# Grouped attention of a fused transformer kernel: query tiles, dense sums, output halves and the last value blocks are made and evicted in other units

## The reference

```python
GROUPS, HPG, KVC = (4, 4, 128)
q = jnp.einsum('bsh,he->bse', x, w_q).reshape(b, sq, GROUPS, HPG, KVC)
kv = jnp.einsum('bsh,he->bse', x, w_kv)
k, v = jnp.split(kv, 2, axis=-1)
scores = jnp.einsum('bqgpd,bkgd->bgqpk', q, k) * SCALE
scores = jnp.where(causal[None, None, :, None, :], scores, -jnp.inf)
probs = jax.nn.softmax(scores, axis=-1).astype(x.dtype)
ctx = jnp.einsum('bgqpk,bkgd->bqgpd', probs, v).reshape(b, sq, HEADS * KVC)
return jnp.einsum('bse,eh->bsh', ctx, w_dense)
```

## Time and profile before

| What | us |
|---|---|
| median of 3 runs | 998.9 (996.7 to 1003.71) |
| the profiled execution's own time | 998.63 |
| its span, first to last instruction | 996.6 |
| grouped attention in it, first scores to last unit's exponentials | 597.0 to 919.3 |
| PE, DVE, ACT busy over the span | 899.9, 744.6, 577.8 |
| granted TensorE clock, mean | 0.991 |

### The profile page before, as it was taken

The page is one execution under the profiler, slowest core; times in us unless marked ns, Lnnn a source line. Parts: engine busy times, 40 slices in busy tenths (PEclk is TensorE's granted clock), DMA queues, the critical chain, the costliest instruction groups (busy, mean ns, idle before and its releaser), DMA issues. The chain is left out here.

```text
span 996.6 us, 19557 instructions
## 1 busy us (share of the span) xinstructions
PE 899.9 (90%) x7309; PEld 601.5 (60%) x7334; DVE 744.6 (75%) x1803; ACT 577.8 (58%) x1102; POOL 173.7 (17%) x131
## 2 busy tenths in 40 slices
PE   3999989999999999999998988899999989998897
PEld 2787743334433433468876765676666766766686
DVE  7846877888888888245468666888888888888654
ACT  5534223566666766744446546767676666766263
POOL 4010130052344145000014500000000000000154
PEclk9999999999999999999999999999999999999999
DMA  5020343453255330203101003667776676766101
GB/s 117 1 88 0 110 122 61 77 104 70 57 107 92 66 77 24 66 1 112 58 1 43 0 1 64 128 120 119 118 122 119 107 132 114 122 123 122 25 1 43
DMA packets 176918, 75.60 MB, mean 76 GB/s; under 512 B 154648, under 2 KB 172744, under 8 KB 175304
## 3 DMA queue, kind: packets, MB, share of 16 engines
q1 hardware_dynamic: 176824, 74.36, 36.7%
HBM read 30.53 MB, written 5.85 MB: 37 GB/s over the span
## 5 line engine op out<-in xcount | busy, mean ns | idle before, releaser
L1010 ACT ACTIVATE PT<-bank 128x512 f32<-128x512 f32 (+2 forms) x320 | 154.4, 559 | 101.9 <-PE bank L1419 83.8
L1908 DVE CUSTOM_DVE_ANT_0 bank<-bank,stripS 128x128 f32<-128x128 f32 (+1 forms) x224 | 129.8, 604 | 28.1 <-PE bank L1343 27.0
L1614 PE MATMUL pair<-KH,QH 128*128 128x512 f16 (+3 forms) x576 | 115.3, 328 | 30.4 <-DVE QH L2019 17.4
L1087 ACT ACTIVATE P<-pair,nm 128x1024 f32<-128x1024 f32 (+7 forms) x128 | 94.5, 738 | 80.9 <-DVE nm L2051 80.7
L1658 PE MATMUL bank<-PT,VH 128*128 128x128 f16 x1728 | 117.7, 219 | 2.9 <-DMA PT<-PS 2.9
L1658 PEld LDWEIGHTS bank<-PT,VH 128*128 128x128 f16 x1728 | 99.4, 98 | 22.5 <-issue 15.7
L1343 PE MATMUL bank<-KT,QT 96*128 96x512 bf16 (+2 forms) x336 | 103.0, 331 | 10.3 <-DVE MX L1908 8.4
L767 POOL TENSOR_TENSOR rstd<-veps,mhalf 128x4 f32<-128x4 f32 x12 | 12.2, 1020 | 557.3 <-DVE veps L1765 557.3
L2077 DVE SCALAR_TENSOR_TENSOR PS<-P,rec,PS 128x1024 f16<-128x1024 f32 (+7 forms) x128 | 102.8, 804 | 5.9 <-ACT PS L1109 4.1
L1822 DVE TENSOR_TENSOR hf<-sil,bank 128x512 f32<-128x512 f32 x64 | 43.9, 686 | 83.6 <-PE bank L1167 52.4
L2047 DVE TENSOR_REDUCE mx<-pair 128x1 f32<-128x1024 f32 (+7 forms) x128 | 96.0, 750 | 7.8 <-PE pair L1616 7.7
(11 more groups left out here) (185 smaller groups left out, 1753.8 us busy)
## 6 DMA issues: line engine op xcount, KB each, us to landing
KT<-qk_dram SPq DMA_DIRECT2D x21, 192.0 KB
stripS<-band_rows SPq DMA_DIRECT2D x28, 128.0 KB, 2.1
qk_dram<-parts SPq DMA_DIRECT2D x12, 256.0 KB, 2.2
stripT<-seq_dram SPq DMA_DIRECT2D x27, 88.0 KB, 8.4
q_raw<-w_gu SPq DMA_DIRECT2D x4, 512.0 KB, 10.1
w_raw<-w_dense SPq DMA_DIRECT2D x2, 1024.0 KB, 6.9
w_raw<-w_q SPq DMA_DIRECT2D x2, 1024.0 KB, 4.8
PT<-PS SPq DMA_TRANSPOSE x128, 3.6
```

The costliest lines, as they stand in the source:

```text
L1010: act.activation(PT[:, n % 4, hs[0]:hs[-1] + 1, 0:ni], src, ACT.Exp).then_inc(s["s2_exp"], 1)
L1087: act.activation(exps(n), pair[n % 2][:, 0:P * (ib + 1)], ACT.Exp, bias=nm1[:, n % 2:n % 2 + 1], scale=SCALE1, accum_out=den1[:, n % 2:n % ...
L1614: ins = pe.matmul(out, QH1[:, h % 2, l, P * ib:P * (ib + 1)], KH1[:, r, h // (H1 // GR), HALF * c:HALF * c + nj], start=(i == 0), stop=(i ...
L1908: dve.tensor_tensor_reduce(out, out, stripS[:, h, HALF - nj:HALF], 1.0, LOWEST, ALU.add, ALU.max, mx).then_inc(s["s1_max"], 1)
```

## The change

Only the places of work in the grouped attention's loops change; no instruction is added or removed.

- `Q_AT` becomes (0, 2): PE makes the query tiles in units 0 and 2 mod 8, ACT copies them in units 1 and 3, DVE takes their low halves in units 3 and 5 (`q_at(n - 3)`; it was n - 1).
- Dense products move to PE units 4, 6 and 12 mod 16, two of them in unit 12. DVE sums them in units 5, 7 and 13.
- The copy of an output half stays in ACT's units 1 and 5, but behind the exponentials. Its low half moves on DVE two units later, to 3 and 7 mod 8, but for the last two.
- The last four value blocks go one to a unit: PE iterations 0 to 3, ACT and DVE iterations 1 to 4.

```diff
-        Q_AT = (1, 5)
+        Q_AT = (0, 2)
         HI_LAG, LO_LAG, PV_LAG, CT_LAG = 1, 2, 5, 6
-        DENSE_FROM = TB + TB // 2 + CT_LAG + 1
-        DENSE_AT = (0, 4, 8, 9)
+        DENSE_FROM = TB + TB // 2 + CT_LAG + 2
+        DENSE_AT = {0: (0,), 2: (1,), 8: (2, 3)}
@@ def dense_at(n)
-            return [(k // (2 * TB), DENSE_AT.index(k % (2 * TB)))] if 0 <= k and k % (2 * TB) in DENSE_AT else []
+            return [(k // (2 * TB), c) for c in DENSE_AT.get(k % (2 * TB), ())] if k >= 0 else []
+
+        def ct_low_at(n):
+            return [q for q in range(STEPS // 4) if n == 4 * q + 3 + CT_LAG + (2 if q < STEPS // 4 - 2 else 0)]
@@ scalar engine, for n in range(-1, LAST)
+                    if 0 <= n < STEPS:
+                        scores(n)
+                    if 1 <= n < 5:
+                        keys_high(KV_AHEAD + n - 1)
                     if 0 <= n - CT_LAG < STEPS and (n - CT_LAG) % 4 == 3:
                         q = (n - CT_LAG) // 4
@@
-                    if n in (0, 1):
-                        keys_high(KV_AHEAD + 2 * n)
-                    if 0 <= n < STEPS:
-                        scores(n)
-                    if n in (0, 1):
-                        keys_high(KV_AHEAD + 2 * n + 1)
@@ tensor engine
-                    if n < 1:
-                        for t in range(KV_AHEAD + 2 * (n + 1), KV_AHEAD + 2 * (n + 2)):
-                            keys_values(t)
+                    if 0 <= n < 4:
+                        keys_values(KV_AHEAD + n)
@@ vector engine
-                    if n in (0, 1):
-                        for t in range(KV_AHEAD + 2 * n, KV_AHEAD + 2 * n + 2):
-                            keys_low(t)
+                    if 1 <= n < 5:
+                        keys_low(KV_AHEAD + n - 1)
@@
-                    if n >= 1:
-                        for h, c in q_at(n - 1):
+                    if n >= 3:
+                        for h, c in q_at(n - 3):
                             queries_low(h, c)
-                    if 0 <= n - CT_LAG < STEPS and (n - CT_LAG) % 4 == 3:
-                        q = (n - CT_LAG) // 4
+                    for q in ct_low_at(n):
                         dve.wait_ge(s["ct_hi"], q + 1)
```

## The result

The changed kernel takes 974.93 us (median of 4 runs, 970.63 to 976.3) against 999.26 in the same job; the ratio of the two is 0.9745, with a 95% interval of 0.9697 to 0.9793. It is faster; 972.0 was forecast, in a range of 965.5 to 985.0. The profiled execution took 976.21 us, its span is 974.3.

A forecast was written before the change was run, and what follows sets the result against it. PE's own work, 36.3 us per two heads, was taken as the floor, with waits deciding. Gains of 1.1 + 3.4 + 21.7 + 1.4 - 1 = 26.6 from 998.63 gave 972 us, range 965.5 to 985, chance 0.60.

The forecast's parts named there:

- The floor: Grouped attention, two heads: PE's own work is 36.3 us of a 40.13 us period; order alone gains at most 3.8.
- one stall: Loop of the opening 8-block scores: DVE is 0.5 late, 4.76 against PE's 4.56, so 0.2 us a period.
- The tie at the opening scores: Every second head: loop of unit 6's exponentials about 3.0 us, PE's own work there 3.0 too.
- The three stalls: PE's waits before scores each period, two for query tiles (1.27, 1.35) and one for exponentials (1.17 us): all go.
- My first rival: DVE keeps waiting for ACT's query tile copies, 0.95 four times a period: gain 2.7 a period, 979 us; chance 0.15.
- The output copy: ACT's copy behind two dense products delays unit 12's halves: hidden by 0.4 us, otherwise up to 1.9 a period.
- My rival: Output copy behind two dense products costs its full 1.9: gain 1.7 us a period, 984 us; chance 0.14.
- Transposes that wait for a unit three back: Units 26, 74 and 122: the ring delays the transpose, which lands as PE arrives, 0.1 us each.
- The microsecond that I held back for ties: Taken off the summed gains for ties and transposes: 1 us given back.
- Units 8 to 24: Start of grouped attention after the first head: from 37.9 to 34.5 us, gain 3.4 (bounds 2.4 and 4.5).
- The tail: Unit 124's low half comes 16.2 instead of 17.6 us behind the last head's opening scores: gain 1.4 (0 to 1.5).
- The first head: Value blocks one to a unit, exponentials some 2 us sooner: gain 1.1 us (bounds gain 4.4, loss 1.5).

The follow-up runs named there:

- e1: Changed kernel with the first query tile of heads 1 to 15 made twice on PE: 995.31 us, ratio to the kernel before 0.9951.
- e2: Changed kernel with one more 3-block row maximum on DVE in unit 5 of each head: 973.31 us, ratio to the kernel before 0.9737.
- e6: Changed kernel with a query tile's low half taken by DVE in the unit in which ACT copies it: 1015.87 us, ratio to the kernel before 1.0167.
- e5: Changed kernel with ACT's copy of an output half back ahead of the exponentials: 973.08 us, ratio to the kernel before 0.9732.
- e7: Changed kernel with the fourth dense product moved from PE's unit 12 to 13, its sum to DVE's unit 14: 981.71 us, ratio 0.9819.
- e3: Kernel before the change with only the query tiles moved: 980.85 us, ratio to the kernel before 0.9821.
- e4: Changed kernel with transposed blocks at fixed places, none reusing that of a unit less than four back: 971.65 us, ratio to the kernel before 0.9718.
- e12: Changed kernel again, with no edit, in a later job: 974.23 us, ratio to the kernel before 0.9758.
- e8: Changed kernel with the last four value blocks as before the change, two in each of two iterations: 973.88 us.
- e9: Changed kernel with an output half's low half taken by DVE in the unit in which ACT copies it: 985.76 us, ratio 0.9872.
- e10: Changed kernel with only the query tiles put back as before: 992.94 us, ratio to the kernel before 0.9947.
- e11: Changed kernel with e4's places and, in iterations 1 to 4, value-block copies behind ACT's high halves, their low halves behind DVE's: 971.67 us, ratio 0.9726.

## Why the prediction was right

**The floor.** 36.3 was computed as the period less the waits, with ends corrected by 0.16 each, and 0.2 was added for one stall. Measured: 36.43, of which 0.17 is that stall, so PE's own work is 36.26. e1 and e2 show that PE is the bound. The stall is where the prediction put it: from the opening scores at 712.45 the maximum comes at 714.47, 2.02 later, 0.46 more than in the other head (0.5 was forecast), and the loop to the 7-block scores at 717.17 takes 4.72 (4.76 forecast) against 4.54 in the other head (4.56). The tie at the opening scores went PE's way in every steady head.

**The three stalls.** They went as written: the query tile fills the 4.26 us loop, the low half two units earlier frees the opening scores. What I hadn't valued is how much the lag of two units carries. My first rival (DVE keeps waiting for ACT's copies, 2.7 gained a period) is what e6 does with one line, and its price was far too low: not 0.95 four times, but 1.6 to 1.7, until the kernel is slower than before. (The 33.6 us of DVE work in that rival's sum stand in no row; by the 34.1 of rows 2 it comes to 2.2 gained a period.)

**The output copy.** The step that called it hidden by 0.4 us was right, and e5 shows that even its place mattered not at all. What I didn't see is the wait on the dense product. My rival named the values product as what holds the copy; in e7 it is the dense product, whose operand the copy overwrites.

**Terms that were mis-sized.** (1) Transposes that wait for a unit three back: 0.1 each was put at three places. At unit 26 PE waited not at all, at unit 74 1.23, at unit 122 1.07, as before (1.09; this is also the 1.1 of rows 3, which the prediction names beside the tail's 2.9 as if it were another wait). The transpose of unit 74 was issued at 782.48, when unit 71's values product was done, and its blocks were used at 788.06, 5.6 us later, where the ones of 26 and 122 had landed after 4.0. The microsecond that I held back for ties covers most of this, which is luck: it was not put there for a slow landing. (2) Units 8 to 24: 2.7 instead of 3.4. Here PE still waits 0.47 and 0.39 for exponentials and 0.45 for a transpose, and ACT 0.50 and 0.31 for transposes ahead of high halves; these waits for transposes stood in no term. With the query tiles alone (e3) the gain here was 3.6. (3) The tail: the low half of unit 124 is earlier by what was forecast, but its transpose took 4.4 us from the end of the low half to the values product (894.84 to 899.25), against 3.8 before, so 0.9 came of 1.4. It landed as fast as before (3.8 us), but was issued 0.6 after its low half, behind the transpose of unit 123, which queued behind the one that the ring held back; in e4 it is issued at once.

```profile
893.84 1.00 DVE L2076 SCALAR_TENSOR_TENSOR PS<-P,rec,PS 128x768 f16<-128x768 f32 x1
```

```profile
899.25 1.18 PE L1658 MATMUL bank<-PT,VH 128*128 128x128 f16 x18 [1.49 <-DMA PT<-PS]
```

(4) The first head: 1.2 for 1.1, with every value block's low half waiting 1.1 to 2.0 us for ACT. The scores of unit 6 came 16.34 us after the first ones (16.5 forecast, 17.26 before), but the hit at the end of the head rests on a drop of the clock that fell into it, as in the kernel before; it is in part luck.

**The sum** for the grouped attention was 26.6 and is 25.8. The rest of the distance to 972 in the profile is the 3.5 us lost in layer 0, which no step of the prediction held.

**The rule weighed.** The Trainium skill, Perfetto Trace Analysis, Optimization Strategy, says that a gap that repeats on the engine that should be saturated can mean too little SBUF or PSUM. Here the pairs of banks stayed at two and the visible gaps went from 3.31 us a period to none: the measurement decides against that cause for this kernel. The wait at 788 does not repeat, and e4 mends it within the same 24 blocks of transposed probabilities. The other section of the Trainium skill's Perfetto Trace Analysis, Identifying the Most-Contended Engine, judges PE by weight loads and by MFU, the share of its peak arithmetic. By weight loads alone (27.70 of 36.43 is 76%, against DVE's 93%) it still names DVE, while e1 and e2 show PE to be the bound; MFU was not worked out here or in the prediction.

## What to carry to other kernels

Where engines with in-order queues alternate long and short units, put side work where the engine that makes it is short, and let each later engine take it up two units on rather than in the same one (here ACT one unit after PE, DVE two after ACT): the same move without the second lag was slower than no move at all. Before placing anything, write down the bound engine's own work for a period (period less its waits); if the side work fits inside a loop that this engine waits out anyway, it is free, and the gain ends at that sum. Look at what frees a buffer as well as at what fills it: the dense product under the output copy and the ring of transposed blocks were waits for a place, though the second only hurt where a transpose was slow as well. And before a difference of a microsecond is put down to an edit, compare the granted clock of the stretch.

## What the runs showed of the hardware

**The clock ahead of the change.** The granted clock of TensorE between 130 and 142 us, in layer 0's attention, differs between kernels whose instructions there are the same. Busy times of this stretch, with the clock third from the end, for the kernel before, the changed one and e12:

```profile
130.00:142.00 12.00, 10.88 (x96) 5.52 (x96) 9.27 (x13) 2.45 (x4) 5.97 (x6) 0.86 0.55 158
```

```profile
130.00:142.00 12.00, 11.15 (x87) 4.43 (x86) 7.79 (x10) 2.33 (x4) 5.97 (x6) 0.57 0.52 158
```

```profile
130.00:142.00 12.00, 11.01 (x86) 4.32 (x78) 7.73 (x10) 2.29 (x4) 5.97 (x6) 0.57 0.53 158
```

PE's list of instructions is the same in the kernel before and the changed one up to the start of the grouped attention. A share of 0.57 means that most of this stretch ran at the lower of the clock's two levels, 1.2 GHz: DVE's instructions, level with those before at 130 us, are 3.5 us behind them at 145, and that is nearly all of the grouped attention's delay. The fourteen profiles fall into three groups: 1.00 in the stretch and the first maximum at 596.7 to 597.5 (e1, e2, e4, e7), 0.86 and 598.4 to 599.1 (eight, the kernel before among them), 0.57 and 602.0 (the two of the changed kernel). The same kernel's runs without a profile speak against its being a mark of this kernel: at a mean granted clock of 0.991 to 0.994 they take 970.6 to 974.2 us, at 0.985 and 0.986, the level of the two profiles, 976.2 to 978.1, and other kernels too have runs at 0.985 and under (e8, e9, e10, e11). So the two profiles most likely caught the same lower level twice; where in the unprofiled runs the clock was lower, nothing on record shows.

**Two prices for the same matmuls.** Six matmuls of 512 columns take 1.37 us behind a group of the same kind and 1.48 behind the 16-bit scores, up to the group that follows (the changed kernel and e1). A sum that moves groups about should use the price for the neighbours that they will have.

**Transposes under load.** The DMA share of a period rose from 0.63 to between 0.76 and 0.86, more than the 0.69 that the shorter period alone gives, while the median landing time stayed (3.7 us after 3.6 before). Single landings did not stay: of the sixteen transposes of 7-block units most land after 4.0 to 4.1 us in both kernels, but four took 5.2 to 5.6 after the change (units 10, 34, 74, 114) and two 5.5 and 6.0 before it (34, 74). What they wait for there, no run shows.
